# Two rows of a triangular solve per step, roots ahead of reciprocals, and keys copied by ScalarE, in a Macaron block with delta-rule attention

## What is computed

```
h = silu(lin(x, w1)) * lin(x, w2)          # 256 -> 1024, ternary weights
h = gelu(lin(h, h1)); h = gelu(lin(h, h2)) # 1024 -> 1024
ffn = lin(h, w3)                           # 1024 -> 256

k = k / max(norm(k), 1e-6)                 # 16 heads of 16
def step(S, (q_t, k_t, v_t, beta_t)):      # over 1024 tokens
    S = S + outer(beta_t * (v_t - S k_t), k_t)
    return S, S q_t
```

## Time and profile before

| | |
|---|---|
| median of 3 runs | 1988.28 us (1987.21 to 1988.53) |
| the profiled execution, its own time | 1994.27 us |
| its span, first to last instruction | 1992.5 us |
| mean granted clock of TensorE over the span | 0.976 |
| busy: PE, PEld | 1824.4 us, 938.1 us |
| busy: DVE, ACT, POOL | 1227.2 us, 908.4 us, 1270.9 us |

### The profile page before, as it was taken

How to read it: one execution, slowest core, us unless ns; L and a number is a source line. 1 busy time by engine, 2 the same in 40 slices (tenths; PEclk the granted TensorE clock), 3 DMA queues, 4 the chain that set the end, 5 groups by cost and what they waited for, 6 DMA issues and landing times.

```text
span 1992.5 us, 25609 instructions
## 1 busy us (share of the span) xinstructions
PE 1824.4 (92%) x8610; PEld 938.1 (47%) x8610; DVE 1227.2 (62%) x3384; ACT 908.4 (46%) x1498; POOL 1270.9 (64%) x1409
## 2 busy tenths in 40 slices
PE   5999989989999998998999879999999899999979
PEld 2445444545445453554545435545444454555424
DVE  4237776667747774677737676577747674676510
ACT  4463453443454435445364353553454445354252
POOL 5465695486746866468647685486736867478452
PEclk9999899999999989999999999999999999999989
DMA  6200000000000000000000000000000000000000
GB/s 211 90 1 1 1 1 1 1 1 1 1 0 22 1 1 22 1 1 1 1 22 1 1 1 1 22 1 1 1 1 1 1 1 11 0 12 1 1 11 11
DMA packets 4448, 22.88 MB, mean 11 GB/s; under 512 B 608, under 2 KB 608, under 8 KB 2784
## 3 DMA queue, kind: packets, MB, share of 16 engines
q1 hardware_dynamic: 4320, 21.26, 3.0%
HBM read 17.06 MB, written 4.19 MB: 11 GB/s over the span
## 4 chain that ended last, share of the span: by engine, by line
PE 55%; DVE 18%; POOL 17%; issue 5%; ACT 4%; DMA 0%; DVEq 0%; POOLq 0%; SPq 0%; ACTq 0%
PE ffn_bank L1044 31%; POOL hid_lo L538 6%; POOL hid L547 5%; PE att_bank L1065 5%; PE att_bank L1087 5%; DVE state_bank L885 4%; PE att_bank L1077 4%; DVE terms L883 4%; PE ffn_bank L1027 3%; POOL pairs L570 2%; PE state_bank L1095 2%; DVE roots L769 2%; DVE O_in L841 2%; POOL pairs_lo L577 2%; PE att_bank L1104 1%
## 5 line engine op out<-in xcount | busy, mean ns | idle before, releaser
L1044 PE MATMUL ffn_bank<-hid_hi,w_sb 128*128 128x512 f16 x2304 | 887.3, 385 | 20.7 <-ACT hid L661 13.0
L1044 PE MATMUL ffn_bank<-hid_lo,w_sb 128*128 128x512 f16 x2304 | 886.9, 385 | 0.0
L538 POOL TENSOR_TENSOR hid_lo<-hid,hid_hi 128x512 f16<-128x512 f32 x384 | 441.8, 1165 | 310.9 <-ACT hid_hi L645 310.7
L570 POOL TENSOR_TENSOR pairs<-KQ 128x32 f32<-128x32 f32 (+14 forms) x496 | 323.1, 667 | 146.0 <-PE att_bank L1077 80.2
L1044 PEld LDWEIGHTS ffn_bank<-hid_hi,w_sb 128*128 128x128 f16 x2304 | 236.7, 103 | 282.1 <-issue 38.6
L1044 PEld LDWEIGHTS ffn_bank<-hid_lo,w_sb 128*128 128x128 f16 x2304 | 228.2, 99 | 266.4 <-issue 52.4
L674 ACT ACTIVATE hid<-ffn_bank,par_sb 128x512 f32<-128x512 f32 x256 | 162.1, 684 | 351.7 <-PE ffn_bank L1044 351.4
L645 ACT CAST hid_hi<-hid 128x512 f16<-128x512 f32 x384 | 224.3, 620 | 107.4 <-POOL hid L547 107.1
L577 POOL TENSOR_TENSOR pairs_lo<-pairs,pairs_hi 128x32 f16<-128x32 f32 (+15 forms) x248 | 171.6, 694 | 132.3 <-ACT pairs_hi L697 132.0
L885 DVE TENSOR_REDUCE state_bank<-terms 128x8 f32<-128x16 f32 (+14 forms) x960 | 226.9, 236 | 33.0
L1027 PE MATMUL ffn_bank<-xn_hi,w_sb 128*128 128x512 f16 x512 | 199.2, 389 | 37.3 <-POOL xn_lo L524 19.8
(11 more groups left out here) (90 smaller groups left out, 2069.3 us busy)
## 6 DMA issues: line engine op xcount, KB each, us to landing
NK<-in_w SPq DMA_DIRECT2D x11, 1024.0 KB, 4.5
X<-in_x SPq DMA_DIRECT2D x8, 512.0 KB, 3.6
out<-X SPq DMA_DIRECT2D x8, 512.0 KB, 2.6
wqkvb_sb<-in_wqkvb SPq DMA_DIRECT2D x1, 1024.0 KB, 4.8
wout_sb<-in_wout SPq DMA_DIRECT2D x1, 256.0 KB, 5.1
par_sb<-in_par SPq DMA_DIRECT2D x1, 24.0 KB, 1.9
```

Of the source, the lines that this page charges most:

```text
L538: pool.tensor_tensor(hid_lo[layer % 2][:, m, :], hid[:, u % 3, :], hid_hi[layer % 2][:, m, :], ALU.subtract).then_inc(hid_lo_ready, 1)
L570: pool.tensor_tensor(packed(pair(pairs, q), w), later, half(KQ[:, 0, :], h)[:, :, :, 0:w], ALU.mult).then_inc(pairs_made if is_split(q) el ...
L1044: mm = nc.tensor.matmul(ffn_ps(off, j), weight(name, kk, 2 * pair + i), v[:, kk, :], start=kk == 0 and part == 0, stop=kk == KT_FF - 1 and ...
```

## The change

Four edits come together.

1. *Layout.* The columns of a slab are ordered by chunk, then tile of features, sequence and token (before: by tile, pair of sequences, chunk). The views lose a dimension; sizes stay. ACT writes projections through `tile_of`, in runs of 64.
2. *Two rows per step.* A step solves rows 2m and 2m+1 with one multiply and one reduce over 2 x 8 x (2m+2) elements, 8 steps for a chunk. The term from the state now lies in u itself with a coefficient 1, and the odd row must not need the even one's result, so `take_dots` puts the even row into each odd row from t = 3 on when it is made: two more DVE instructions of 32 x 2m elements in front of the multiply by beta. The fixed ones and zeros are filled in once at the start, by 48 fills. The copy at L876 falls away.
3. *Layer norms.* ACT takes the root straight from the bank with the offset as its bias; DVE takes the reciprocal afterwards and multiplies at once. `ln_offset` is gone, the root's tick is earlier, attention's two roots stand together, and the quarters of the reciprocal are taken after rows 11 to 14 instead of 9 to 12.
4. *Keys.* `make_kz` moves from POOL to ACT, at the same tick, as four copies of 32 partitions x 128 elements into a Kz zeroed once.

```diff
-LN_ATT = dict(sum=129, mean=131, square=142, sq_sum=143, var=146, root=164, apply=168, y_root=172, low=174)
+LN_ATT = dict(sum=129, mean=131, square=142, sq_sum=143, var=146, root=148, apply=165, low=172)
-                root=at + (15 if c >= 0 else 12), apply=at + (20 if c >= 0 else 32), low=at + (22 if c >= 0 else 34))
-SOLVE_LN = {8: "offset", 9: 0, 10: 1, 11: 2, 12: 3}
+                root=at + 8, apply=at + (20 if c >= 0 else 32), low=at + (22 if c >= 0 else 34))
+SOLVE_LN = {11: 0, 12: 1, 13: 2, 14: 3}
...
                 if part == "root":
-                    act.wait_ge(ln_inverted, i * 1 + 1)
-                    r = roots[:, 1 if kind == "att" else 0, :]
-                    act.activation(r, r, ACT.Sqrt).then_inc(ln_rooted, 1)
+                    act.wait_ge(ln_filled, i * 2 + 2)
+                    if kind == "att":
+                        act.activation(roots[:, 1, :], ln_bank[:, :], ACT.Sqrt, bias=eps[:, 1:2])
+                    act.activation(roots[:, 0, :], ln_bank[:, :], ACT.Sqrt, bias=eps[:, 0:1]).then_inc(ln_read, 1)
...
+            def make_kz(s, c):
+                if c >= 1:
+                    act.wait_ge(dstate_ready, s * CH + c)
+                act.wait_ge(k_turned, s * CH + (c + 1))
+                for q in range(QUADS):
+                    rows = slice(q * 32, (q + 1) * 32)
+                    act.copy(Kz[rows, :, q * 32:(q + 1) * 32], KTr[rows, c % 2, :, :]).then_inc(kz_ready, 1)
...
             def take_dots(s, q):
+                    m, odd = divmod(t, 2)
+                    rows = nk_rows(m, h)
+                    if odd and m:
+                        elim = packed(qk_u[:, 0:HRUNS * 2 * m], 2 * m)
+                        nc.vector.tensor_tensor(elim, rows[:, 0, :, 0:2 * m], ps[:, :, 2 * m:t].to_broadcast([P, HRUNS, 2 * m]), ALU.mult).then_inc(row_mixed, 1)
+                        dve.wait_ge(row_mixed, mixed(s, h, m, 1))
+                        nc.vector.tensor_tensor(ps[:, :, 0:2 * m], ps[:, :, 0:2 * m], elim, ALU.add).then_inc(row_mixed, 1)
+                        dve.wait_ge(row_mixed, mixed(s, h, m, 2))
+                    nc.vector.tensor_tensor(rows[:, odd, :, 0:t], ps, half(beta[:, :], h)[:, :, t:t + 1].to_broadcast([P, HRUNS, t]),
                                             ALU.mult).then_inc(att_read_v, 1)
...
-                step(nc.vector.tensor_copy(u_view[:, :, :, 0], four(terms[:, 0, :, 0:1])[:, :, :, 0]))
-                for t in range(1, C):
+                for m in range(STEPS):
                     if c == 0:
-                        take_dots(s, DOT_KK[0] + t - 1)
+                        for t in (2 * m, 2 * m + 1):
+                            if t:
+                                take_dots(s, DOT_KK[0] + t - 1)
...
-                    step(nc.vector.tensor_tensor(four(terms[:, t, :, 1:t + 1]), nk_row(t, c), u_view[:, :, :, 0:t], ALU.mult))
+                    step(nc.vector.tensor_tensor(part, rows, known.to_broadcast([P, 2, GB, w]), ALU.mult))
                     last_step()
-                    step(nc.vector.tensor_reduce(u_view[:, :, :, t], four(terms[:, t, :, 0:t + 1]), AX.X, ALU.add))
+                    step(nc.vector.tensor_reduce(u_view[:, :, 2 * m:w].rearrange("p g v -> p v g"), part, AX.X, ALU.add))
```

More of the change, by code:

```diff
@@ L70 @@
 QK = [(t, t + 1) for t in range(C)]
-KK_AT = [HRUNS * t * (t - 1) // 2 for t in range(C + 1)]
+STEPS = C // 2
+NK_AT = [HRUNS * 2 * m * (m + 1) for m in range(STEPS + 1)]
 DOTS = HALVES * (len(KK) + len(QK))
@@ L109 @@
 E_OUT = 160
-LN_ATT = dict(sum=129, mean=131, square=142, sq_sum=143, var=146, root=164, apply=168, y_root=172, low=174)
-LN_ATT_FIRST = dict(sum=-18, mean=-15, square=-13, sq_sum=-11, var=-9, root=-4, apply=-2, y_root=4, low=8)
-LN_SECOND = dict(sum=46, mean=48, square=50, sq_sum=51, var=54, root=60, apply=70, y_root=75, low=80)
+LN_ATT = dict(sum=129, mean=131, square=142, sq_sum=143, var=146, root=148, apply=165, low=172)
+LN_ATT_FIRST = dict(sum=-18, mean=-15, square=-13, sq_sum=-11, var=-9, root=-8, apply=-2, low=8)
+LN_SECOND = dict(sum=46, mean=48, square=50, sq_sum=51, var=54, root=56, apply=66, low=72)
 QUARTERS = 4
@@ L568, in make_pairs @@
                         pool.wait_ge(att_filled, s * ATT_U + (U_DOT[q - PAIR_BUFFERS] + 1))
-                later = half(KQ[:, 1 if of_q else 0, :], h)[:, :, :, t:t + 1].to_broadcast([P, GP, 2 * HCH, w])
-                pool.tensor_tensor(packed(pair(pairs, q), w), later, half(KQ[:, 0, :], h)[:, :, :, 0:w], ALU.mult).then_inc(pairs_made if is_split(q) else pairs_ready, 1)
+                later = half(KQ[:, 1 if of_q else 0, :], h)[:, :, t:t + 1].to_broadcast([P, HRUNS, w])
+                pool.tensor_tensor(packed(pair(pairs, q), w), later, half(KQ[:, 0, :], h)[:, :, 0:w], ALU.mult).then_inc(pairs_made if is_split(q) else pairs_ready, 1)
             def low_pairs(s, q):
@@ L711, in attention @@
                         act.wait_ge(resid_taken, s * CH + (c + 1))
-                        act.copy(at_chunk(O[:, :], c), four(retr(c)[:, :, C:2 * C])).then_inc(att_read_s, 1)
+                        act.copy(at_chunk(O[:, :], c), retr(c)[:, :, C:2 * C]).then_inc(att_read_s, 1)
+                    if e == E_RETR[c] + 6:
+                        make_kz(s, c)
             def alone(call, job, second):
@@ L934, in alone @@
                         convert(i)
+                    dve.wait_ge(w_ready, W_PIECES)
+                    for h in range(HALVES):
+                        for m in range(STEPS):
+                            rows = nk_rows(m, h)
+                            nc.vector.memset(rows[:, 0, :, 2 * m:2 * m + 1], 1.0).then_inc(units_set, 1)
+                            nc.vector.memset(rows[:, 0, :, 2 * m + 1:2 * m + 2], 0.0).then_inc(units_set, 1)
+                            nc.vector.memset(rows[:, 1, :, 2 * m + 1:2 * m + 2], 1.0).then_inc(units_set, 1)
                     ln_center(second)
-                    ln_invert(second)
+                    ln_recip(second)
                     ln_norm(second)
```

172 lines of the change are left out of this document (78 added, 94 removed).

## The result

The changed kernel takes 2006.85 us (median of 4 runs, 2003.16 to 2011.92) against 1988.12 us (4 runs, 1987.21 to 1988.53): a ratio of 1.0091, 95% interval 1.007 to 1.0112. On another chip it was 2006.66 us against 1993.32 us, 1.0077 (1.0058 to 1.0095). It is slower, by 0.8 to 0.9%, where 0.8% faster was forecast. The profiled execution took 2011.92 us, its span is 2010.2 us and the granted clock 0.966.

What follows compares the result with a forecast made beforehand. PE, 92% busy, was taken as the bound, so time could come only from its standstills. Terms -27.3 + 0.7 + 20.0 - 6.9 + 6.8 - 12 + 3 - 0.7 = -16.4 us gave 1972 us, range 1950 to 1998.

Steps and rivals of the forecast that it cites:

- The solve's and the mixing's prices: On DVE: a chunk's solve falls from 7.91 to 5.40 us; mixing costs 5.77 us per half slab, 6.25 with waits.
- Chunk 0, +20.0: Chunk 0 of each slab: DVE has 3.74 us more work, partly hidden in waits for dots; +20.0 us over eight slabs.
- The clock, -6.9 + 6.8: PE's clock: two low stretches behind stalls go, -6.9 us; half the slabs get a new one of 1.7 us, +6.8.
- Chunks 1, 2 and 4 to 7, -27.3: PE's twenty waits for Uz in these chunks go: 23.9 us, and 3.4 us hidden behind them, together -27.3 us.
- Chunk 3, +0.7: Chunk 3: mixing costs 3.45 us against 2.51 saved; its three waits grow 0.2 us each, +0.7 us.
- Norms, -0.7, with 0 for the root inside a solve: Layer norms: -1.4 us for first and last, +0.7 for attention's first; the 13 inside solves cost 0, 13 us kept for range.
- Keys, -12 + 3: Keys moved to ACT: 14 chunks wait 0.85 us less for POOL or ACT, -12 us; ACT's copies cost +3 us.
- Rival C: Chunk 0: nothing hides, low clock follows all eight stalls, ACT eats the keys' relief; +10.0 us, 1998 us, chance 0.17.
- B: Rival: chunk 0 isn't late, its DVE instruction count staying about equal; -43.2 us, 1945 us, chance 0.13.

Runs made afterwards that it cites:

- E12: The changed kernel itself, run once more on another chip: 1.0077 of the kernel before.
- E4: Changed kernel without the 14 mixing instructions of the first half, all in chunk 0 (computation left incomplete): 1971.56 us, 0.9907 of the kernel before.
- E11: Changed kernel without any mixing in either half, new norms kept (computation left incomplete): 1952.67 us, 0.9802 of the kernel before.
- E14: Changed kernel without any mixing and with the layer norms of before (computation left incomplete): 1945.28 us, 0.976 of the kernel before.
- E1: Changed kernel with the keys copied by GpSimd again, all else as changed: 2004.94 us, 1.0121 of the kernel before.
- E7: Kernel before with only the new layout and ScalarE's key copies; one row per step, old norms: 1979.48 us, 0.9946 of the kernel before.
- E5: Kernel before with only the new layout; one row per step, old norms, keys by GpSimd: 0.9984 of the kernel before.
- E3: Changed kernel with one row per step and no mixing; layout, norms and keys as changed: 1980.67 us, 0.9979 of the kernel before.
- E2: Changed kernel with the layer norms of before, all else as changed: 2014.82 us, 1.0137 of the kernel before.
- E9: Changed kernel with old norms, one row per step in chunks 0 to 3, second half mixed in gaps of NK: 1980.51 us, 0.9939 of the kernel before.

## Why the prediction was wrong, step by step

*The solve's and the mixing's prices* were right: 5.30 us for 5.40, 5.94 us for 5.77. DVE's busy time came out at 1167.8 us, not 1145, because the sum took the saving of 161 us from busy and idle time together. Of busy time alone: 1227.2 - (447.3 - 311.4) + 95.0 - 22 + 4.1 for the fills = 1168.4.

*Chunk 0, +20.0*: right in size. Uz waits there grew by 17.6 us (22.3 - 4.7) and those for NK by 4.1 (7.5 - 3.4), 21.7 in all. It hid a little less than assumed, 3.3 us a slab longer where 20.0 / 8 = 2.5 was taken; slab 4 hid the most, 0.9 us longer with 1.1 forecast.

*The clock, -6.9 + 6.8*: the step that failed. I took 1.7 us for each low stretch from the one row at 610.88 us, for half the slabs, with 13.6 us as the bound. There are seven, 29.5 us together and 4.2 us each, against 1.7 us in all before. That is +27.8 and not +6.8 (+22.5 in E12's execution). The bound came from one mild example, although the other row beside it (5.2 us behind 3.33 us) showed that a stretch can cost three times that. The gain was off too. Outside chunk 0 the stalls before cost 6.0, 5.2, 1.7 and 1.7 us of speed (behind 226, 699.85, 946 and 1344 us, 14.6 in all; the last, behind a stall of 1.68 us, is one that the prediction missed when it said that the short waits leave the clock alone). The second and third are gone, but the changed kernel has 2.5, 4.7, 1.7 and 3.2 us behind 236, 293, 871.6 and 1361 us, 12.1 in all, so -2.5 and not -6.9. That makes +25.3 us, of which the mean clock of the span shows 20.5, and the means over all executions 21.9 (63.5 - 41.6): in windows of 5 us over the whole span, the low stretches behind neither kind of stall withhold about 33 us before and 27 after. E4 shows that the low stretches behind chunk 0 come from the 14 instructions (3.4 us there), but also that about half of that speed is then withheld elsewhere. What the forecast had as -0.1 us for the clock was 22 us; the other terms, -16.3 together, came to -7.2 apart from the clock. The clock's error alone turns the forecast of -16 us into +6; the other 9 us come on top.

*Chunks 1, 2 and 4 to 7, -27.3*: half of it came. Their waits fell from 23.9 to 11.1 us. Of the seventeen waits in chunks 4 to 7 (20.4 us) four are left (6.0 us), each with a norm's reciprocal in the solve; the others went, as forecast. 8.7 of the 11.1 us, in chunks 1, 2, 4 and 6, stand behind a wait for a root inside the solve, which belongs to the norms' step below. "That covers all seventeen waits" was too much by its own numbers as well: the longest, 3.33 us, was above the 3.23 saved, and 0.60 us of it is left. *Chunk 3, +0.7*: +3.5. The mixing in chunks 1 to 3 is also dearer than its busy time: E4 has 19.8 us more span than E11, 14.2 us of it in PE's busy time (1823.2 - 1809.0), so part of it is again the clock (12.2 us by the table of all executions).

*Norms, -0.7, with 0 for the root inside a solve*: wrong in sign where DVE is early, 0.4% or 8 us (E14 to E11), with waits for the root like the one at 286.63 us. The 0 rested on the new slack of 3.2 us; a wait of 3.13 us, then four quarters and the last two steps, uses it up. The waits for Uz grew by 12.6 us (22.4 - 9.8), near the 13 us kept for the range, but the loss stands in the clock: 13.3 us more withheld, against 6.1 us saved in the rest. Where these 6.1 us come from I have not traced.

*Keys, -12 + 3*: right in size. 7.9 us of waits by E1, 7.6 us of time by E7 over E5. In the table of the changed kernel they hardly show (51.4 against 53.2). Against E5 instead of the kernel before they do: the four rows are 56.7 us there with POOL's keys, 3.5 more than before the layout, and 51.7 in E7. That hid_lo rose from 7.1 to 14.4 us is the norms' (14.7 in E3, 6.2 in E7), but it is not a loss: pairs_lo, gate and hid fall by as much, so that E2 with the old norms has 52.9 us in the four rows.

Rival C named the mechanism, nothing hides and each chunk 0 has a low stretch behind it, and gave 1998 us. It fell short because its eight stretches of 1.7 us are 13.6 us, where 27.8 were measured; and it had the keys' relief eaten by ACT, which E1 does not bear out. The opposite rule, B, that fewer instructions decide, fell: DVE has 721 instructions fewer (2663 against 3384), 59 us less busy time, and the kernel is slower. The Trainium skill ("VectorE: DVE Perf Modes", section "Rules for kernel authors") advises the lower count for chained operations; here a mixing instruction of 448 elements takes 608 ns, and its place in chunk 0 decides.

What stays open: why the clock stayed at 1.00 behind the 2.88 us at 1307.40, in both executions, when it fell behind shorter stalls; in the rows it isn't decided by the stall's length, and behind the first chunk 0 the same stall went either way.

## What to carry to other kernels

Saved busy time counts in the stage where it is saved: 161 us less in 64 chunks and 100 us more in 32 left 7 us of gain apart from the clock, since the added part fell where the engine was already last, and the low clock behind the longer stalls took three times that. Where the bound engine has a clock that falls after stalls, price a stall by what the worst seen low stretch behind one withheld, not by the mildest. Take the withheld speed, one minus the clock times the span, out of every execution before two kernels are compared: what is left hardly scatters, and it shows whether an edit lost its time in the work or in the clock. Before an operation is put in the middle of a chain, follow its supplier back one queue further (here the root, behind ACT's cast, behind POOL's product).

## What the runs showed of the hardware

A multiply or add on VectorE with both inputs in SBUF (L884 and L886 of E9) took between 182 ns and 6.83 us, where the ones that read one input from PSUM kept to 221 ns for 64 and 608 ns for 448 elements in the changed kernel. The longest one lay beside instructions of GpSimd without a gap between them. The Trainium skill ("SBUF — State Buffer", section "Who interferes with whom") says that VectorE reads its second SBUF input through an interface shared with GpSimd, held for a whole instruction. The trace agrees that the two hinder each other, and shows more: VectorE's multiply spans seven whole instructions of GpSimd (from 661.33 to 667.71 us), not one. That the shared interface is the cause of this length is the reading that fits; no run tests it by itself.

Executions of one kernel differ by TensorE's clock and by little else: over 23 executions of the kernel before, the span ran from 1978.1 us at a granted clock of 0.986 to 2001.3 us at 0.974, while the span less the withheld speed kept between 1945.9 and 1952.8 us.
